# Where and in what layout the softmax sums of a tuned attention block are inverted

## The reference, cut to what matters

```python
h = _layernorm(x) * (1 + ca) + sa
qkv = h @ W_qkv + b_qkv                      # 16 heads, q, k, v of 32 each
q, k = _apply_rope(q, cos, sin), _apply_rope(k, cos, sin)
att = einsum('bhqd,bhkd->bhqk', q, k) / sqrt(32)
att = softmax(where(causal, att, -1e9), axis=-1)
y = einsum('bhqk,bhkd->bhqd', att, v)
x = x + ga * (y @ W_proj + b_proj)
h = _layernorm(x) * (1 + cb) + sb            # then the second half
```

## Time and profile before

| | |
|---|---|
| Median of 3 runs | 3443.67 us (3442.83 to 3448.5) |
| The profiled execution | 3444.86 us, span 3443.1 us |
| PE busy | 3061.1 us, 89% of the span |
| DVE busy | 2675.1 us, 78% |
| ACT busy | 1762.3 us, 51% |
| POOL busy | 1714.1 us, 50% |
| Granted TensorE clock, mean | 0.944 |
| Reciprocals of `dsum` (L888) on DVE | 252, 234.9 us |

### The profile page before, as it was taken

The page is one execution under the profiler, slowest core; times in us unless marked ns, Lnnn a source line. Parts: engine busy times, 40 slices in busy tenths (PEclk is TensorE's granted clock), DMA queues, the critical chain, the costliest instruction groups (busy, mean ns, idle before and its releaser), DMA issues.

```text
span 3443.1 us, 58785 instructions
## 1 busy us (share of the span) xinstructions
PE 3061.1 (89%) x21664; PEld 1166.0 (34%) x21664; DVE 2675.1 (78%) x4326; ACT 1762.3 (51%) x3411; POOL 1714.1 (50%) x1257
## 2 busy tenths in 40 slices
PE   3799999899989899899998999999888998999895
PEld 1333333334342433424333242433324333242221
DVE  4686777896768788897877878798886878878577
ACT  3416565656645554665544555565544555455451
POOL 2404444563536465473644636465562655636354
PEclk8769999999999999999999999999999999999897
DMA  5302120312031210313113031311203112021022
GB/s 204 98 21 52 31 55 27 83 34 73 13 100 38 72 50 23 93 41 82 38 53 88 25 91 32 81 46 44 77 31 106 44 38 72 26 75 44 24 91 71
DMA packets 180872, 205.25 MB, mean 60 GB/s; under 512 B 21460, under 2 KB 137428, under 8 KB 179428
## 3 DMA queue, kind: packets, MB, share of 16 engines
q1 hardware_dynamic: 180584, 201.50, 20.3%
HBM read 114.09 MB, written 36.50 MB: 44 GB/s over the span
## 4 chain that ended last, share of the span: by engine, by line
PE 44%; DVE 27%; issue 11%; ACT 5%; DVEq 5%; POOLq 3%; POOL 2%; DMA 2%; SPq 1%; ACTq 0%
DVE mpart L872 12%; PE ring L1112 10%; PE ps_out L1162 9%; PE ps_scores L1148 7%; PE ps_den L1179 4%; PE ps_scores L1086 4%; PE ps_den L1185 3%; DVE wk L916 3%; PE ring L1134 3%; DVE dsum L888 2%; ACT xw L660 2%; DVE half L849 2%; DVE wk L914 2%; DVEq L842 2%; DVE x L962 2%
## 5 line engine op out<-in xcount | busy, mean ns | idle before, releaser
L712 ACT ACTIVATE prob<-ps_scores 128x512 f32<-128x512 f32 (+3 forms) x2560 | 1270.1, 538 | 1141.4 <-PE ps_scores L1151 576.2
L872 DVE TENSOR_REDUCE mpart<-ring 128x1 f32<-128x512 f32 (+3 forms) x2560 | 1401.5, 600 | 303.3 <-PE ring L1115 153.3
L510 POOL TENSOR_TENSOR psum<-prob 128x1024 f32<-128x1024 f32 x360 | 868.3, 2433 | 319.0 <-PE ps_den L1179 160.2
L1112 PE MATMUL ring<-qk 96*128 96x512 f16 (+3 forms) x2560 | 894.6, 370 | 127.2 <-DVE mpart L872 115.7
L1148 PE MATMUL ps_scores<-qk 98*128 98x512 f16 (+3 forms) x2560 | 884.4, 359 | 96.5 <-DVE v L854 49.5
L1162 PE MATMUL ps_out<-prob,v 128*32 128x512 f32 (+3 forms) x5120 | 617.5, 555 | 0.0
L1112 PEld LDWEIGHTS ring<-qk 96*128 96x128 f16 x2560 | 240.8, 99 | 982.0 <-DVE mpart L872 713.9
L496 POOL TENSOR_TENSOR xw<-xw,turn 128x512 f32<-128x512 f32 x128 | 203.4, 1589 | 596.4 <-ACT xr L662 553.4
L1148 PEld LDWEIGHTS ps_scores<-qk 98*128 98x128 f16 x2560 | 250.7, 100 | 408.6 <-ACT prob L712 199.8
L1086 PE MATMUL ps_scores<-hT,wg 128*128 128x512 f16 x1536 | 345.1, 381 | 3.5 <-POOL hT L501 3.5
L660 ACT ACTIVATE xw<-ps_scores,bqk 64x512 f32<-64x512 f32 x256 | 175.2, 684 | 300.7 <-PE ps_scores L1086 165.1
(11 more groups left out here) (121 smaller groups left out, 2454.1 us busy)
## 6 DMA issues: line engine op xcount, KB each, us to landing
qk<-half SPq DMA_DIRECT2D x384, 128.0 KB, 3.2
turn<-in_rope_dram SPq DMA_DIRECT2D x64, 512.0 KB, 4.3
xs<-in_L_attn_x_dram SPq DMA_DIRECT2D x124, 256.0 KB, 2.8
attn_out_T<-ot SPq DMA_DIRECT2D x63, 256.0 KB, 2.1
otin<-attn_out_T SPq DMA_DIRECT2D x30, 512.0 KB, 4.7
out_dram<-x SPq DMA_DIRECT2D x60, 256.0 KB, 2.1
wg<-w_qkv_halves SPq DMA_DIRECT2D x16, 768.0 KB, 5.4
qk<-in_L_wmod_dram SPq DMA_DIRECT2D x1, 6144.0 KB, 27.1
```

What stands on the lines that cost most here:

```text
L510: pool.tensor_tensor(psum2[:, p], prob[:, s % 3, p], prob[:, (s + 1) % 3, p], ALU.add).then_inc(pair_sum, 1)
L712: act.activation(prob[:, s % 3, p, h % 2, 0:w], ps_scores[(HG * s + h) % NBK][:, 0:w], ACT.Exp, scale=SCALE).then_inc(exp_done, 1)
L872: dve.tensor_reduce(mpart[:, h, qt, kc:kc + 1], ring[n % NBK][:, 0:w], AX.X, ALU.max).then_inc(ring_free, 1)
L1112: mm = pe.matmul(ring[n % NBK][:, 0:w], qk[0:R, G % 2, 0, h, qt * P:(qt + 1) * P], qk[0:R, G % 2, 1, h, kc * QC:kc * QC + w], start=True, ...
```

## The change

`dsum` is no longer inverted where it stands. SP issues four DMAs (`spread_sums`), each of which takes the first of a head's 32 equal rows (512 numbers) and lays it over that head's 32 partitions, 16 numbers on each, in a new tile `dense` of 128 x 16. DVE inverts `dense` with one reciprocal of 16 elements a partition. SP stores it to a DRAM tensor `rows_d` (`store_inverses`) and loads it back into `dsum`, each head's row broadcast to its 32 partitions (`load_inverses`). POOL's multiply now waits for that load. For chunk 3 the DMAs, the reciprocal and the multiply stand in the QKV stage that follows; the rest stands one step earlier than before. For chunks 0 to 2 the rest stands one step later. The planner's `vector_load` counts 0.5 in one step where it counted 2.4 in each of four.

```diff
-    FAST = {"leave": 0, 0: 1, 1: 1, 2: 2, 3: 2, "norm": 2, "high": 3, "low": 4, "store": 5}
-    LATE = {0: 2, 1: 2, 2: 3, 3: 3, "norm": 3, "high": 4, "low": 4, "store": 5}
-    SLOW = {"leave": 0, 0: 1, 1: 2, 2: 3, 3: 4, "norm": 4, "high": 5, "low": 6, "store": 7}
+    FAST = {"leave": 0, "spread": 0, "recip": 1, "rows": 1, "norm": 2, "high": 3, "low": 4, "store": 5}
+    LATE = {"high": 2, "low": 3, "store": 4}
+    LAST = {"recip": 1, "rows": 1, "norm": 2, "high": 3, "low": 4, "store": 5}
+    SLOW = {"leave": 0, "spread": 0, "recip": 2, "rows": 3, "norm": 5, "high": 6, "low": 7, "store": 8}
...
-        load = 2.4 * sum(leaving(s, part, False) is not None for part in range(TPC))
+        load = 0.5 * (leaving(s, "recip", False) is not None)
...
+    rows_d = nc.dram_tensor("sum_inverses", (HG, QC), F32, kind="Internal").ap()
...
+        dense = sb("dense", [P, QC // HS], F32)
...
# SP
+                    if c == 1 and G >= 2:
+                        load_inverses(G - 2, NC_ - 1)
                     if G < NG * B - 1 or c < NC_ - 1:
                         load_turn(NC_ * G + c + 1)
+                    if c == 0 and G >= 2:
+                        spread_sums(G - 2, NC_ - 1)
                     if c == 0 and before is not None:
                         maxima_rows(before, before % 2)
                     stack_halves(G, c, 0)
+                    if c == 0 and G >= 2:
+                        store_inverses(G - 2, NC_ - 1)
...
+                        cq = leaving(s, "spread", bool(own))
+                        if cq is not None:
+                            spread_sums(NG * b + g, cq)
+                        cq = leaving(s, "rows", bool(own))
+                        if cq is not None:
+                            store_inverses(NG * b + g - (cq == NC_ - 1), cq)
+                            load_inverses(NG * b + g - (cq == NC_ - 1), cq)
...
+            def spread_sums(G, cq):
+
+                sp.wait_ge(sums_left, NC_ * G + cq + 1)
+                with nc.allow_non_contiguous_dma(reason="one of 32 equal rows a head, 64 B a partition"):
+                    for h in range(HG):
+                        sp.dma_start(dense[h * HS:(h + 1) * HS, :],
+                                     dsum[h * HS:h * HS + 1, :].rearrange("o (j i) -> o j i", j=HS)).then_inc(dense_ld, 16)
+
+            def store_inverses(G, cq):
+                sp.wait_ge(recip_done, NC_ * G + cq + 1)
+                sp.dma_start(rows_d.rearrange("h (j i) -> (h j) i", j=HS), dense[:]).then_inc(rows_st, 16)
+
+            def load_inverses(G, cq):
+                sp.wait_ge(rows_st, 16 * (NC_ * G + cq + 1))
+                sp.dma_start(dsum[:], rows_d.rearrange("h (o q) -> h o q", o=1).to_broadcast([HG, HS, QC])).then_inc(
+                    rows_ld, 16)
...
# POOL
-                pool.wait_ge(recip_done, TPC * (NC_ * G + cq + 1))
+                pool.wait_ge(rows_ld, 16 * (NC_ * G + cq + 1))
...
+                            if c == 2 and G > 0:
+                                out_norm(G - 1, NC_ - 1)
...
# DVE
                     cosines(G, c, 0)
+                    if c == 0 and G >= 2:
+                        out_reciprocal(G - 2, NC_ - 1)
                     turned_sum(G, c, 0)
...
-                dve.wait_ge(sums_left, NC_ * G + cq + 1)
-                cols = slice(part * P, (part + 1) * P)
-                dve.reciprocal(dsum[:, cols], dsum[:, cols]).then_inc(recip_done, 1)
+                dve.wait_ge(dense_ld, 16 * HG * (NC_ * G + cq + 1))
+                dve.reciprocal(dense[:], dense[:]).then_inc(recip_done, 1)
```

17 lines of the change are left out of this document (8 added, 9 removed).

## The result

The change makes the kernel slower: 3466.7 us (median of 4 runs, 3462.2 to 3472.8) against 3444.5 us for the kernel before on the same chip (4 runs, 3442.8 to 3448.5). The ratio is 1.0058, with a 95% interval of 1.0046 to 1.0070. Forecast were 3385 us, and 9 chances in 10 of faster. The profiled execution took 3463.5 us, its span 3461.7.

The account below looks back on a forecast made before the run. PE alone paces groups 0, 1 and 3; in head groups PE and DVE block each other, and tail groups leave PE idle. 61 + 6 - 8 = 59 us gained gave 3385 us, range 3315 to 3438.

Parts of the forecast that it names:

- The relief, 61 us: Attention steps beside the old reciprocals: three quarters of 81 us of PE idle come back, 61 us.
- everything that PE waits for is DVE's backlog: Rival, attention: the 81 us and half of the 93 outside come back, less 8: 119 us, 3325; chance 20%.
- tails and heads keep their stalls: Rival, attention: only a third of the 81 us comes back, 9 to 20 us gained, about 3430; chance 17%.
- The planner, +6: Attention: units move into the relieved steps, easing the others; 6 us gained, ends -10 and 46.
- The first hop: Attention: row copies into `dense` land 2.2 us after issue, DVE may wait 0.4 to 1.3 us; cost taken as 0.
- The rival named as the slower side: Attention: `dense` lands late, PE stops some 1.5 us for 45 chunks, 67 us; about 3452; chance 8%.
- Nobody waits: Attention: rows are back about 10 us after the copy, POOL asks after some 13 us; no cost.
- 134 to 135 us as before: Sign to check: attention stages of groups 0, 1 and 3, paced by PE alone, keep their length.
- SP has nothing urgent behind its new waits: SP's queue in attention: the loads behind the waits are asked for two steps later; no cost.
- like the loads of 256 KB, 2.8 us: Broadcast load of the inverses into `dsum`: lands in 2.8 us, as loads of 256 KB do.
- by some tenths: QKV stage: the load's issue moves the rope table's by 0.6 us; it may be slightly late, DVE still busy.
- POOL's multiply in the QKV stage, 8 us: POOL and DVE hold each other up: 0.6 us in each of 14 stages, 8 us cost, ends 0 and 18.

Follow-up runs that it names:

- e5: Kernel before, with DVE inverting only 16 of 512 columns of each chunk, no hops, planner's old costs: 3396.5 us, ratio 0.9854.
- e4: Kernel before, with DVE inverting only 16 of 512 columns of each chunk, no hops, planner's new cost of a reciprocal: 3436.7 us, ratio 0.9970.
- e14: Changed kernel with the planner's costs of before and nothing else: 3471.6 us, ratio 1.0077.
- e2: Changed kernel with POOL's multiply of chunks 0 to 2 four steps behind the leave, not five: 3449.3 us, ratio 1.0006.
- e16: Changed kernel with the spread issued behind the tail's loads in each attention step: 3457.2 us, ratio 1.0029.
- e13: e11 with the planner's old costs: 3408.2 us, ratio 0.9888.
- e15: e13 with the spread behind the tail's loads and chunk 3's load of the inverses behind the loads of step 0: 3383.7 us, ratio 0.9814.
- e10: Changed kernel, but chunk 3's load of the inverses, in the QKV stage, brings only 16 of 512 columns: 3418.3 us, ratio 0.9919.
- e8: e2 with the broadcast load into dsum as four DMAs, one for each head's 32 partitions: 3436.5 us, ratio 0.9971.
- e11: e8 with chunk 3's load behind the QKV stage's last half copies and its multiply, cast and difference where they stood before the change: 3413.2 us.
- e6: Changed kernel with the broadcast load into dsum as four DMAs, one for each head's 32 partitions: 3453.4 us, ratio 1.0019.
- e12: Changed kernel with chunk 3's multiply, cast and difference where they stood before the change, its load left in the QKV stage: 3462.1 us.

## Why the prediction was wrong

It forecast the gain from the relief about right and priced the ways in which the new route loses it at nearly nothing.

- **The relief, 61 us:** nearly right. e5 has it alone: 51 us. The guess that three quarters of the idle beside the reciprocals comes back was high by some 10 us. The rival by which everything that PE waits for is DVE's backlog is out: its sum was 119. For it I had written that DVE has no idle to speak of in the head groups; by the earlier trace rows it idles 39.0 of 469.7 us there, as much as PE. The rival by which tails and heads keep their stalls (9 to 20 us) is out by e5; e4's 10 us match its size, but the planner's placement makes them.
- **The planner, +6:** small in the changed kernel, where the new costs are worth 5 us (e14), at the edge of what can be told. In e4, which is the prediction's own pair of 61 + 6 without the hops, they lose 40, far outside the end of -10; why there alone is open.
- **The first hop:** right. 1.7 us to land, 25.9 us of waits in all, 3.8 of them outside group 15. The rival named as the slower side, `dense` late and PE stopped in every chunk, did not happen. The kernel is slower by another way.
- **"Nobody waits":** failed, and this is one of three steps that failed. The rows were in time, but I asked only when they come back and not what stands ahead of the multiply on POOL at its new step. In steps 17 and 29 that is the sum of a pair, 4.7 us; step 9, chunk 0's, has none. It cost 16 us of attention (e2). Groups 0, 1 and 3, "134 to 135 us as before", showed it: they went to 137.3, 138.2 and 136.8, and e2 puts them back to 133.7, 134.6 and 133.8.
- **"SP has nothing urgent behind its new waits":** failed. In the groups with six tails the load for the tail of step 14 is asked for in step 12, where chunk 1 leaves. The two steps of lead that I counted on were already its landing time: `otin` takes 4.6 us. It cost 12.1 us in the three steps, 10 by the runs (e16), and 14.7 in step 14 from e13 to e15.
- **The load into `dsum`, "like the loads of 256 KB, 2.8 us", and the table late "by some tenths":** failed, and here lies most of the miss. Of the QKV stages' 43.8 us this load makes 36.3 (e10), 2.6 us in each of 14. I had counted only the 0.6 us of its issue against the table behind it; in the stage ahead of group 4 POOL had the table 4.1 us later after the load's issue than in e10. Two things were left out. The larger is the load's place: a quarter of a megabyte, with its issues, stood ahead of a load that POOL and DVE wait for. With the load behind the stage's last copies and the multiply out of the stage the QKV sum falls from 596.3 to 556.9 (e8 to e11). The smaller is its shape: I took the duration from a row of the same size and not of the same access pattern, and as four DMAs it gives back 7.3 of the 36.3 us (e6). The Trainium skill says outright (DMA: Bandwidth & Descriptors, Rules for kernel authors) that an outermost dimension under 16 confines the whole DMA to at most that many engines, and I had not held the new access pattern against it.
- **POOL's multiply in the QKV stage, 8 us:** compatible. With the wide load gone and the multiply kept the 15 stages take 7.5 us more than before (e10), though part of that may be the narrow load; with the wide load in place, leaving the multiply out gives only 2.2 (e12). My upper end was 18, and I had put it down to the port rule of the Trainium skill (SBUF — State Buffer, the two separate sides). The trace agrees with the rule: DVE's L876 takes 1.75 us at 997.21, begun under POOL's multiply, and 0.69 us at 993.70, begun just ahead of POOL. But I had worked the 18 out wrongly. A sum at 980.34 that waits for a multiply from 979.70 to 980.97 waits 0.63 us and not 1.28, so 8.8 us in 14 stages, close to the 8 taken and to the 7.5 measured.

Added up, with sizes from the runs: -51 for the relief, +16 for the multiply behind the pair, +10 for the tail's load, +36 for the wide load and +7.5 for the rest of the QKV stage give +19; measured are +22, or 20 by the ratio. That they agree so well is partly chance. Three sizes, which overlap and which no run takes apart, stand outside this sum: the planner's new costs gain 5 us (e14), the wide load's removal also gave 10.3 us of attention time (e10), and steps 34 and 35 of the tail groups gain 22.9 us over e5.

Mended one by one, the same idea gives 3383.7 us. That this lies beside the forecast of 3385 is luck. e15 has neither the planner's 6 us, as it has the old costs, nor the 8 us of the multiply, which it does in the attention steps. The relief alone comes to 3396.5, and the 13 us between are mostly the gain in steps 34 and 35, which I had not forecast. What failed is that three costs of the route stood at nothing in the sum without having been looked up.

## What to carry to other kernels

Price a new DMA by its access pattern and by what is queued behind it, not by the landing time of another of its size: here 256 KB held up the table behind them by 4.1 us as one transfer and still by 2.8 us as four that land in 2.0 us each. When an instruction moves by one step, list what its in-order engine does ahead of it there, for POOL and for SP as for the others. If a gain comes out smaller than its term, do the relief alone on the chip first: the difference between that run and the full change is the net price of the route, and it can be hunted down stage by stage. Net, for the route can gain something too, as here in steps 34 and 35.

## What the runs showed of the hardware that I had not expected

Two stalls of PE cost more than their length. After 3.08 us of idle the twelve projection matmuls of group 4, step 16, took 4.22 us, and the window over them has a granted clock of 0.64:

```profile
1079.80:1084.10 4.30, 4.23 (x13) 1.67 (x14) 1.12 (x2) 0.00 (x0) 0.45 (x1) 0.64 0.18 65
```

Before, the same twelve took 2.75 us:

```profile
1059.87 2.75 PE L1134 MATMUL ring<-wp,otin 128*128 128x512 f16 x12
```

The window over them, 1059.8 to 1062.7 us, has a granted clock of 1.00. A mean of 0.64 says that most of that stretch ran at 1.2 GHz, not 2.4. So 1.5 us come on top of the 3 us, and the same happens behind the late `otin` (4.45 us for 2.75, after 2.54 us of idle, at a granted clock of 0.62 from 1679.3 to 1683.8 us).
